# A graph-attention and mixture-of-experts layer: experts' numbers loaded one per tile behind the first product, and 64 neighbouring rows per partition in the combination

## What is computed

```python
x = x + gnn(layernorm(x), adj)          # attention over the graph's edges, 128 -> 128
x = x + ffn(layernorm(x)[None])[0]      # 16 experts, the best two per row

# ffn
probs = softmax(x @ gate_w + gate_b)
top_probs, top_idx = top_k(probs, 2);  top_probs /= sum(top_probs)
hidden = silu(x @ w1[e]) * (x @ w2[e])  # 128 -> 256, for each expert e
y = sum over the two experts of  prob * (hidden @ w3[e])   # 256 -> 128
```

## Time and profile before

| | us |
|---|---|
| median of 3 runs | 1891.75 (1890.79 to 1894.92) |
| the profiled execution | 1883.58 |
| its span, first to last instruction | 1881.8 |

### The profile page before, as it was taken

How to read it: one execution, slowest core, us unless ns; L and a number is a source line. 1 busy time by engine, 2 the same in 40 slices (tenths; PEclk the granted TensorE clock), 3 DMA queues, 4 the chain that set the end, 5 groups by cost and what they waited for, 6 DMA issues and landing times.

```text
span 1881.8 us, 24594 instructions
## 1 busy us (share of the span) xinstructions
PE 1535.9 (82%) x8112; PEld 854.9 (45%) x8113; DVE 1470.3 (78%) x2024; ACT 1278.7 (68%) x1620; POOL 604.0 (32%) x840
## 2 busy tenths in 40 slices
PE   5587899898899889889988988899995058888880
PEld 5454444454454445434444543455553035555560
DVE  7799999999989999998999899889874113433344
ACT  4899899698779878887987888677563024444440
POOL 6500012221341225133213604222325634444450
PEclk9999999999999999999999999999998569999995
DMA  6899687487748757764876676454231142222229
GB/s 196 300 319 320 199 273 243 137 265 238 222 145 277 226 160 249 241 223 138 270 233 189 211 247 222 126 162 146 66 113 44 35 135 64 61 62 59 65 59 271
DMA packets 143075, 339.40 MB, mean 180 GB/s; under 512 B 16962, under 2 KB 64258, under 8 KB 142978
## 3 DMA queue, kind: packets, MB, share of 16 engines
q1 hardware_dynamic: 120784, 303.26, 51.1%
q0 software_dynamic: 11824, 28.50, 4.7%
q10 hardware_dynamic: 10370, 6.38, 1.1%
HBM read 309.57 MB, written 28.51 MB: 180 GB/s over the span
## 4 chain that ended last, share of the span: by engine, by line
PE 34%; DVE 32%; issue 17%; POOL 8%; ACT 5%; DMA 3%; SPq 0%; ACTq 0%; DVEq 0%; POOLq 0%
DVE probs L1196 15%; PE pair L898 15%; DVE ring L1142 13%; PE pair L985 7%; PE pair L885 4%; PE pair L1001 4%; ACT ring L690 3%; PE pair L992 2%; DMA ring<-res_d 1%; POOL xd_d L604 1%; ACT probs L741 1%; POOL ln L565 1%; PE pair L981 1%; POOL numT L574 1%; POOL xd_d L657 1%
## 5 line engine op out<-in xcount | busy, mean ns | idle before, releaser
L898 PE MATMUL pair<-probs,X 128*128 128x512 f32 x2048 | 1013.9, 613 | 1.8 <-ACT probs L741 1.6
L741 ACT ACTIVATE probs<-probs,ebias 128x1024 f32<-128x1024 f32 (+1 forms) x576 | 602.4, 1047 | 264.4 <-DVE probs L1196 263.1
L1196 DVE SCALAR_TENSOR_TENSOR probs<-s1row,ns,pair 128x1024 f32<-128x1024 f32 (+1 forms) x576 | 658.2, 1157 | 65.8 <-PE pair L885 63.6
L1142 DVE CUSTOM_DVE_ANT_0 ring<-urow,ring 128x2048 int8<-128x2048 f16 x256 | 596.4, 2331 | 10.1 <-ACT ring L690 10.0
L690 ACT ACTIVATE ring<-stage,neghalf 128x1024 int8<-128x1024 int32 x512 | 574.8, 1140 | 1.3 <-DMA stage<-in_adj 0.9
L885 PEld LDWEIGHTS pair<-diag,ring 128*128 128x128 fp8e5 x4096 | 266.0, 99 | 485.3 <-DVE probs L1196 254.7
L898 PEld LDWEIGHTS pair<-probs,X 128*128 128x128 f32 x2048 | 347.3, 192 | 220.5 <-issue 215.7
L885 PE MATMUL pair<-diag,ring 128*128 128x128 bf16 x4096 | 327.2, 221 | 147.0 <-DVE probs L1196 120.9
L1417 DVE COPY probs<-pair 128x256 f32<-128x256 f32 x144 | 61.2, 425 | 188.4 <-PE pair L992 180.3
L985 PE MATMUL pair<-ring,probs 128*128 x288 | 167.7, 666 | 42.1 <-issue 41.2
L662 POOL DMA_INDIRECT res_d<-probs x144 | 139.2, 966 | 181.9 <-ACT probs L789 178.2
(11 more groups left out here) (217 smaller groups left out, 839.1 us busy)
## 6 DMA issues: line engine op xcount, KB each, us to landing
stage<-in_adj SPq DMA_DIRECT2D x512, 512.0 KB, 4.3
probs<-xd_d SPq DMA_DIRECT2D x144, 65.0 KB, 1.8
ring<-res_d SPq DMA_DIRECT2D x16, 512.0 KB, 8.7
ring<-in_L_ffn_w SPq DMA_DIRECT2D x2, 2048.0 KB, 12.6
out<-ring ACTq DMA_DIRECT2D x8, 512.0 KB, 7.3
xres<-in_x POOLq DMA_DIRECT2D x7, 512.0 KB, 7.5
s1row<-s_d SPq DMA_DIRECT2D x7, 512.0 KB, 6.8
xmid_d<-xres POOLq DMA_DIRECT2D x7, 512.0 KB, 5.8
```

The source lines that it names most:

```text
L741: act.activation(probs[:, n % PR, 0:wide], probs[:, n % PR, 0:wide], ACT.Exp, bias=ebias[:, j:j + 1], scale=RISE).then_inc(probs_ready, 1)
L898: m = pe.matmul(acc[q][:, lo:hi], X[:, j, :], probs[:, n % PR, lo:hi], start=(j == 0), stop=(j == NT - 1))
L1142: dve.tensor_tensor_reduce(m, urow[:, c * CH:(c + 1) * CH], m, CODE, NO_EDGE, ALU.subtract, ALU.max, part[:, k, c:c + 1]).then_inc(piece_d ...
L1196: dve.scalar_tensor_tensor(out=probs[:, n % PR, 0:wide], in0=s1row[:, q, 0:wide], scalar=ns2[:, j:j + 1], in1=Tp[n % 2][:, 0:wide], op0=AL ...
```

## The change

Two independent edits, with no other change.

First, TensorE reads experts' numbers one at a time (`expert_of`). Those of tile i+1 are read right after `m_h(i)`, ahead of `t_x(i+1)`. In a round of the loop the first tile's number is still read at the head of the round, and the numbers of the two tiles before the round, whose `m_y` is to come, are read again in its first two tiles, so that these have two loads behind `m_h`.

Second, in the combination a partition owns 64 neighbouring rows: row `64 p + t` is partition p's column t, in `xm`, in both halves of `res_d` and in `out`.

```diff
-        out_t = out.rearrange("(t p) d -> p t d", p=P)
+        out_t = out.rearrange("(p t) d -> p t d", p=P)
...
-            sp.dma_start(xm, xmid_t).then_inc(xm_in, 16)
+            sp.dma_start(xm, xmid_d.rearrange("(p t) d -> p t d", p=P)).then_inc(xm_in, 16)
...
-            res_t = res_d[0:2 * N, :].rearrange("(c t p) d -> c p t d", c=2, p=P)
+            res_t = res_d[0:2 * N, :].rearrange("(c p t) d -> c p t d", c=2, p=P)
...
-            def experts_of(i, n):
-                return nc.values_load_multi_w_load_instructions(
-                    tab[0:1, bass.ds(ST + i, n)], engines=(mybir.EngineType.PE,), min_val=0, max_val=E - 1,
-                    skip_runtime_bounds_check_because="every tile of the table belongs to one of the experts")[1]
+            def expert_of(i):
+                return nc.values_load(
+                    tab[0:1, bass.ds(ST + i, 1)], engines=(mybir.EngineType.PE,), min_val=0, max_val=E - 1,
+                    skip_runtime_bounds_check_because="every tile of the table belongs to one of the experts")
...
             with pe.Fori(1, ST // XS - 1) as g:
-                e = experts_of(XS * g - 2, XS + 2)
+                e = {0: expert_of(XS * g)}
                 for u in range(XS):
                     i = XS * g + u
-                    m_h(i, u, e[u + 2])
+                    m_h(i, u, e[u])
+                    if u < 2:
+                        e[u - 2] = expert_of(XS * g + (u - 2))
+                    if u + 1 < XS:
+                        e[u + 1] = expert_of(XS * g + (u + 1))
                     t_x(i + 1, (u + 1) % XS, g + 1 if u + 1 < XS else g + 2)
                     t_h(i - 1, (u - 1) % XS)
-                    m_y(i - 2, (u - 2) % XS, e[u], False)
+                    m_y(i - 2, (u - 2) % XS, e[u - 2], False)
```

More of the change, by code:

```diff
@@ L1006, in _ @@
             pe.wait_ge(w12_in, 32)
-            e = experts_of(0, XS)
+            e = {0: expert_of(0)}
             t_x(0, 0, 1)
@@ L1010, in _ @@
                 m_h(i, i, e[i])
+                if i + 1 < XS:
+                    e[i + 1] = expert_of(i + 1)
                 t_x(i + 1, (i + 1) % XS, (i + 1) // XS + 1)
@@ L1016, in _ @@
             with pe.Fori(1, ST // XS - 1) as g:
-                e = experts_of(XS * g - 2, XS + 2)
+                e = {0: expert_of(XS * g)}
                 for u in range(XS):
                     i = XS * g + u
-                    m_h(i, u, e[u + 2])
+                    m_h(i, u, e[u])
[3 more added lines that the diff above has]
+                        e[u + 1] = expert_of(XS * g + (u + 1))
                     t_x(i + 1, (u + 1) % XS, g + 1 if u + 1 < XS else g + 2)
                     t_h(i - 1, (u - 1) % XS)
-                    m_y(i - 2, (u - 2) % XS, e[u], False)
-            e = experts_of(ST - XS - 2, XS + 2)
-            for i in range(ST - XS, ST + 2):
+                    m_y(i - 2, (u - 2) % XS, e[u - 2], False)
+            first = ST - XS
+            e = {first: expert_of(first)}
+            for i in range(first, ST + 2):
                 if i < ST:
-                    m_h(i, i % XS, e[i - (ST - XS - 2)])
+                    m_h(i, i % XS, e[i])
+                    if i - 2 < first:
+                        e[i - 2] = expert_of(i - 2)
+                    if i + 1 < ST:
+                        e[i + 1] = expert_of(i + 1)
                 if i + 1 < ST:
@@ L1031, in _ @@
                     t_h(i - 1, (i - 1) % XS)
-                m_y(i - 2, (i - 2) % XS, e[i - (ST - XS)], False)
+                m_y(i - 2, (i - 2) % XS, e[i - 2], False)
         @block.vector
```

## The result

| | us |
|---|---|
| before, median of 4 runs | 1892.7 (1890.79 to 1894.92) |
| after, median of 4 runs | 1836.01 (1831.88 to 1838.71) |
| ratio | 0.9686, 95% interval 0.9665 to 0.9707 |
| the profiled execution after, and its span | 1837.41, 1835.6 |

The change takes 56.7 us off, 3.1%. The prediction was 1848 with 1830 to 1872: its sign is right, the time lies in the range, and the gain is 13 us larger than predicted.

The account below looks back on a forecast made before the run. TensorE's chain was taken to bound the experts' stage, with a ten-number load idling each round's head, and DMA the combination. Gains of 36 + 4.5 + 3 = 43.5 us took the median from 1891.75 to 1848, range 1830 to 1872.

Parts of the forecast that it names:

- What bounds the experts' stage: Experts' loop: TensorE's chain throughout; a round loses 3.51 us, 2.50 of it idle at the head during the ten-number load.
- The form 5T - 0.66 for a round's loss: Experts' loop after the first edit: a round's loss for single-load price T, from head, pairs and register operations; 1.34 us forecast.
- the window of 0.83: Steady tile on TensorE: the queue has 0.83 us behind `m_h` before `t_x` is delayed; a lone load is free to T = 0.63.
- I take T = 0.40, between the two bounds: TensorE's load of one number: price T taken as 0.40 us, between 0.25 (words fetched singly) and 0.53 (SyncE's eight numbers).
- The term of 36 us: First edit, experts' stage: 34.7 us back from 16 rounds, and 1.3 for the load before the last eight tiles.
- The second edit, 4.5 us: Combination: 4 KB runs at up to 386 GB/s save between 2.1 and 6.0 us; 4.5 taken.
- `xm`, 3 us: First tiles: the load of `xm` ends 3.5 us sooner, shortening TensorE's 5.0 us wait for a tile; 3 taken.
- The price does not depend on the array's work: Rival on TensorE's loads: with the array at work each single load costs some 2.5 us, ending near 2190; chance 0.10.
- a load first let the array run empty: Milder form of the load-price rival: all of T and the handover lie behind `m_h`, 5.8 us a round, 1921; chance 0.10.
- The clock did not fall: Rival in the experts' loop: the clock keeps falling, half the rounds still lose 0.8 us, 13 us go, 1861; chance 0.12.
- the runs' length changes nothing: Rival on the DMA edit: loads stay at today's rate, 36 us remain, 1856; chance 0.10.
- What would show it: Signs: 178 loads at 0.25 to 0.53 us, rounds about 15 us, no 0.50 clock inside the loop, combination at 350 to 390 GB/s.

Follow-up runs that it names:

- loads_eight: Kernel before, its loop reading eight aligned numbers at a round's head and the two earlier tiles' numbers singly, DMA edit left out: median 1842.76 us, ratio 0.9768.
- carried: Changed kernel with experts' numbers kept in a ring of eight registers from round to round, no load at the head: median 1816.88 us, ratio 0.9630.
- loads_three: Changed kernel, every loop tile reading the number of the tile two before twice behind its first product, beside the next tile's: rounds of 16.82 us.
- loads_only: Changed kernel with the three rearranged layouts put back, so only the first edit: median 1841.61 us, ratio 0.9745.
- rows_only: Kernel before with only the second edit, 64 neighbouring rows per partition: median 1877.88 us, ratio 0.9928.
- runs_1k: Changed kernel with 1 KB instead of 4 KB runs in the first residual's load and the combination's loads and writes: median 1833.47 us, ratio 0.9707.
- xm_early: Changed kernel with SyncE issuing the load of `xm` ahead of its waits for the dispatch: median 1824.73 us, ratio 0.9663.
- carried_xm_early: Changed kernel with both numbers carried in eight registers and the load of `xm` moved ahead of the dispatch: median 1812.32 us, ratio 0.9611.
- loads_ahead: Changed kernel with each tile's number read right ahead of that tile's first product, not behind the previous tile's: median 1830.78 us, ratio 0.9696.

## Why the prediction was right, and what it missed

*What bounds the experts' stage*: the load of ten at the head, 2.50 us, with the restart and the low clock behind it. Right; with the load of ten out of the rounds the idle time at a head is 0.31 us (after), 0.57 (`loads_eight`) or none (`carried`), and the low clock is gone.

*The form 5T - 0.66 for a round's loss*: with the measured T = 0.30 it gives 0.84, and 0.82 was measured. The head's part, T + 0.20, gives 0.50, and 0.51 stands in the chain (0.31 and 0.20). The pairs came out as 0.26 and nothing, where it gives 0.17, 0.07 and 0.10 for register operations. That the sum fits to 0.02 is in part luck: the first pair's 0.26 is nearly all `t_x`'s own 0.32 for 0.11, which the formula has no term for, and the window of 0.83 that it rests on is too narrow, as `loads_three` shows.

*"I take T = 0.40, between the two bounds"*: this is the step that was off. 0.30 was measured, next to my lower bound of 0.25, words fetched one by one. My upper bound, SyncE's 0.53 for eight numbers, would be two pieces of four words by the rule found and says nothing of a single word but that it is less. The term of 36 us became 46.3 (`loads_only`, from the first tile on): 10 of the missing 13 us, 8.5 of them by T, as 5 x 0.10 x 17 rounds and last tiles; behind the last branch 2.6 came back and not 1.3, which is 0.8 more than T explains, and 1.0 stays unexplained.

*The second edit, 4.5 us*: the mechanism was right and the size too small; 8.0. I took the adjacency's 386 GB/s as the best a queue of 4 KB runs can do, and then only part of it. Mixed traffic went at 404. That stretch of the adjacency, though its queue was full, was no ceiling. Of the 13 us that the gain is larger, 10.3 are the first edit's, 3.5 this one's, and `xm` gave 0.5 less than counted.

*`xm`, 3 us*: 2.5 measured to tile 8's transpose, in the way predicted: the tile load shortened, 4.82 to 1.94, the scatter not.

*The rivals.* The price does not depend on the array's work (0.60 and 0.60 for eight words, 2.62 and 2.63 for ten, idle and at work); nor does a load first let the array run empty, for behind a lone load the chain shows nothing. Of the three differences between the 0.78 and the 2.5 us that I listed, the start was the one that mattered, together with the number of words; the eight at 0.78 are the 0.60 of an aligned read and 0.18 that the first read costs more (0.50 for one word against 0.32). The clock did not fall once in the rounds looked at, with pauses of 0.3 us (after) and 0.6 (`loads_eight`). That the runs' length changes nothing is out by `rows_only` (11.7 us less, interval 0.9903 to 0.9953) and by the rates by run length.

*What would show it*: the loads' row and no stretch at 0.50 in the windows of the loop came as written, and TensorE's wait for tile 8 is under 3 us. "Issue" at a head is 0.31 us, under the 0.4 to 0.7 that I gave, and behind a pair 0.02 or none, where I gave 0.2 to 0.6; rounds are 14.4 and not 15; the combination is above the 390 GB/s that I gave as its most. SyncE's last issue comes 17.49 us behind its first where it came 29.96, so 12.5 sooner and not 4. With 1 KB runs (`runs_1k`) it is 23.08, so this too goes with the run's length, but by what is not shown, and my reading of rows 13, that the queue was full, was never tested.

*The profiled execution against the median*: I took the 8.2 us between them to stay as they are. They didn't: the profiled execution after lies 1.4 above its median. This moved the median's prediction by nothing, since the sum is a difference, but whoever compares spans only sees 46 us of 56.

## What to carry to other kernels

Before batching register reads of a table, look at where each batch starts: off a multiple of four words four to ten words cost 2.0 to 3.6 times as much, and keeping a few numbers in registers from round to round may spare the odd start altogether. A sequencer's load of 0.3 us was free once in a steady tile, behind a long product of 0.92 us; three in a tile showed, and so does one (0.31 us and 0.20 for the restart) at a point where the array has nothing queued. When a bound is made of two rows, ask what the operation in each row is made of before taking the middle.

## What the runs showed of the hardware that was not expected

- A load by TensorE's sequencer costs about 0.07 us and 0.25 for each piece; a piece is four words from a start on a grid of four, otherwise one word (0.34 us for four words on the grid, 1.00 off it).
- Runs of 512 B, 1 KB and 4 KB move at 333, 379 and 402 to 404 GB/s in mixed traffic; for 4 KB runs a pitch of 4 or 32 KB made no difference.
- After one and the same pause of 32 us the granted clock rose to 1.00 behind two first products in some executions (`carried`, `xm_early`) and behind three in others (`carried_xm_early`, `loads_ahead`, `loads_three`), some 1.7 us of difference where TensorE's code is the same (`carried` and `carried_xm_early`). What decides it was not found.
- Behind 0.02 us of idle time a transpose took 0.32 us of the chain, where it takes 0.11 behind none.
- The adjacency's stage alone moves the first tile by 10 us between executions: its last product starts at 1436.8 us before and at 1446.9 after.
